# Splitting the weights later within the first four steps of a three-stage kernel on one core

## What is computed

```python
z = rmsnorm(x, norm_in_w) @ pre_w.T
folded = mean of z over 4 neighbouring tokens
gate = sigmoid(Hst @ harm_w.T + harm_b)
gfold = folded * gate
target = style @ style_w.T
cos = sum(l2norm(gfold) * l2norm(target))
cfg_blend = gfold + cfg * (1 + cos) * 0.5 * (target - gfold)
y = concatenate([x, cfg_blend]) @ merge_w.T + merge_b
h = gelu(rmsnorm(y, norm_out_w) @ ffn_w1.T + ffn_b1)
y = h @ ffn_w2.T + ffn_b2 + x
```

## Time and profile before

| what | value |
|---|---|
| device time, median of 3 runs | 1429.6 us (1429.23 to 1430.48) |
| the profiled execution's own time | 1431.61 us |
| its span, first to last instruction | 1429.8 us |
| mean granted TensorE clock | 0.987 |
| busy: PE, DVE, ACT, POOL | 1370.5, 960.7, 1035.9, 911.5 us |

### The profile page before, as it was taken

How to read it: one execution, slowest core, us unless ns; L and a number is a source line. 1 busy time by engine, 2 the same in 40 slices (tenths; PEclk the granted TensorE clock), 3 DMA queues, 4 the chain that set the end, 5 groups by cost and what they waited for, 6 DMA issues and landing times. The chain is left out here.

```text
span 1429.8 us, 30429 instructions
## 1 busy us (share of the span) xinstructions
PE 1370.5 (96%) x10795; PEld 1183.3 (83%) x10795; DVE 960.7 (67%) x2191; ACT 1035.9 (72%) x2703; POOL 911.5 (64%) x855
## 2 busy tenths in 40 slices
PE   7899999997899999999999999999999988999996
PEld 6799999996678887888888788788888777889896
DVE  5876667643776676677667667666755568678763
ACT  5556666565898889889888988988988732476662
POOL 2576666652678768867877876786787620354643
PEclk9899999999999999999999999999999999999999
DMA  5342222111100100110110011011011046145522
GB/s 159 114 129 67 68 67 68 49 45 30 38 9 30 53 23 31 53 45 9 52 46 31 30 53 36 18 53 45 9 45 46 30 148 253 45 104 156 137 35 30
DMA packets 61638, 89.04 MB, mean 62 GB/s; under 512 B 6144, under 2 KB 50992, under 8 KB 58800
## 3 DMA queue, kind: packets, MB, share of 16 engines
q1 hardware_dynamic: 53232, 75.82, 16.3%
q0 software_dynamic: 6144, 8.39, 3.6%
q10 hardware_dynamic: 2112, 2.88, 0.6%
HBM read 61.90 MB, written 25.18 MB: 61 GB/s over the span
## 5 line engine op out<-in xcount | busy, mean ns | idle before, releaser
L1386 POOL TENSOR_TENSOR prob<-prob,share_p 128x512 f32<-128x512 f32 x256 | 271.6, 1067 | 195.6 <-DVE share_p L1493 195.0
L1487 DVE TENSOR_REDUCE shift<-bank 128x2 f32<-128x512 f32 x256 | 164.7, 685 | 186.0 <-PE bank L1103 185.9
L1258 ACT ACTIVATE prob<-bank,shift 128x256 f32<-128x256 f32 x512 | 237.8, 479 | 64.3 <-DVE shift L1487 64.2
L147 PE MATMUL bank<-wqkv_h,rowsT_h 128*128 128x512 f32 x384 | 158.9, 414 | 2.8 <-PEq L311 1.7
L147 PE MATMUL bank<-wqkv_h,rowsT_l 128*128 128x512 f32 x384 | 151.5, 395 | 0.0
L147 PE MATMUL bank<-wqkv_l,rowsT_h 128*128 128x512 f32 x384 | 150.8, 393 | 0.0
L1115 PE MATMUL bank<-ident,prob 128*128 128x128 f32 x1024 | 142.7, 281 | 1.1 <-POOL prob L1386 1.1
L1374 POOL TENSOR_TENSOR landing<-landing,rq 128x512 f32<-128x512 f32 x128 | 131.1, 1046 | 8.4 <-DVE rq L1441 8.4
L1130 PE MATMUL bank<-pT,landing 128*64 128x256 f32 x1024 | 127.1, 388 | 1.7 <-ACT pT L1345 1.7
L1115 PEld LDWEIGHTS bank<-ident,prob 128*128 128x128 f32 x1024 | 109.5, 141 | 21.3 <-POOL prob L1386 3.7
L1258 ACT ACTIVATION_READ_ACCUMULATOR prob<-bank,shift 128x1 f32 x512 | 107.5, 210 | 0.0
(11 more groups left out here) (324 smaller groups left out, 4517.6 us busy)
## 6 DMA issues: line engine op xcount, KB each, us to landing
landing<-in_fc1s SPq DMA_DIRECT2D x6, 1024.0 KB
landing<-in_fc2s SPq DMA_DIRECT2D x6, 1024.0 KB
rows<-in_x SPq DMA_DIRECT2D x16, 256.0 KB, 2.9
xT<-in_xT SPq DMA_DIRECT2D x16, 256.0 KB, 2.7
x_again<-in_x SPq DMA_DIRECT2D x16, 256.0 KB, 2.8
x_rows<-x SPq DMA_DIRECT2D x16, 256.0 KB, 3.1
rows<-x_rows SPq DMA_DIRECT2D x16, 256.0 KB, 3.1
x<-x_rows SPq DMA_DIRECT2D x16, 256.0 KB, 2.9
```

What stands on the lines that cost most here:

```text
L147: last = nc.tensor.matmul(out, a, b, start=(n == 0), stop=(n == 3 * len(ks) - 1))
L1258: last = nc.scalar.activation(prob[at][:, n, :], score_bank[side][:, n * T:(n + 1) * T], ACT.Exp, bias=shift[:, at, n:n + 1], scale=-1.0, ...
L1386: nc.gpsimd.tensor_tensor(prob[at][:, :, :], prob[at][:, :, :], share[:, at, :].unsqueeze(2).to_broadcast([P, TT, T]), ALU.mult).then_inc( ...
L1487: nc.vector.tensor_reduce(shift[:, s % 2 * 2 + side, :], score_bank[side][:, :].rearrange("p (n m) -> p n m", n=TT), AX, ALU.min).then_inc ...
```

## The change

The instructions stay the same in number and in size; their places in the order of two engines change. On ScalarE the high part of piece 1 goes behind the squares of `gf` in step -2, that of piece 2 behind the copies to `xnT` in step -2, and that of piece 3 behind the copies to `xnT` in step -1. On VectorE the low part of piece 1 goes behind the blend in step -2, those of pieces 2 and 3 behind `hn` in steps -1 and 0, and `hbias` behind `bl_l` in step -2. TensorE, GpSimd and SyncE are untouched.

```diff
@@ -557,14 +557,12 @@
                     if at(t, -2):
                         act.wait_ge(gate_sum, 1)
                         nc.scalar.activation(gate[:, :, :], gate[:, :, :], ACT.Sigmoid).then_inc(gate_done, 1)
-                        high_part(act, 1)
-                        high_part(act, 2)
-                    if at(t, -1):
-                        high_part(act, 3)
                     if live(far):
                         wait(act, gf_done, 1, far, 1)
                         wait(act, g_rooted, 1, far - 1, 1)
                         squares(gf, junk_act[:, 1, :, :], g_sums).then_inc(gf_squared, 1)
+                    if at(t, -2):
+                        high_part(act, 1)
                     if live(new):
                         wait(act, xn_T, 1, new, 1)
                         wait(act, folded, 1, new - 1, 1)
@@ -572,6 +570,10 @@
                             last = nc.scalar.activation(xnT[:, k, 0:T], xn_bank[:, k * T:(k + 1) * T], ACT.Copy,
                                                         scale=cols[:, NORM_IN + k:NORM_IN + k + 1])
                         last.then_inc(xnT_out, 1)
+                    if at(t, -2):
+                        high_part(act, 2)
+                    if at(t, -1):
+                        high_part(act, 3)
                     if at(t, -3):
                         load_piece(act, 2)
                         load_piece(act, 3)
@@ -714,19 +716,8 @@
                     if at(t, -2):
                         dve.wait_ge(gate_done, 1)
                         link(nc.vector.tensor_scalar(gate[:, :, :], gate[:, :, :], 0.25, None, ALU.mult))
-                    if at(t, -2):
-                        low_part(dve, nc.vector, 1).then_inc(lo_pool, 1)
-                        dve.wait_ge(setup_done, 3)
-                        dve.wait_ge(tables_in, 32)
-                        for m in range(KT):
-                            last = nc.vector.tensor_scalar(hbias[:, m, :], banks[5][:, m * NB:(m + 1) * NB],
-                                                           cols[:, LN1_B + m:LN1_B + m + 1], cols[:, B_ADA + m:B_ADA + m + 1], ALU.add, ALU.add)
-                        last.then_inc(hbias_done, 1)
                     if at(t, -1):
-                        low_part(dve, nc.vector, 2).then_inc(lo_dve, 1)
                         dve.wait_ge(biases_in, 32)
-                    if at(t, 0):
-                        low_part(dve, nc.vector, 3).then_inc(lo_dve, 1)
                     if live(far):
 
                         wait(dve, pre_done, 1, far, 1)
@@ -797,12 +788,18 @@
                         for i in range(TT):
                             last = nc.vector.scalar_tensor_tensor(blend[:, i, :], trow_b[:, 0:D], mix[:, i:i + 1], gfs[:, i, :], ALU.mult, ALU.add)
                         last.then_inc(blended, 1)
+                    if at(t, -2):
+                        low_part(dve, nc.vector, 1).then_inc(lo_pool, 1)
                     if live(nxt):
                         wait(dve, y_rooted, 1, nxt, 1)
                         wait(dve, h_T, 1, nxt - 1, 1)
                         for i in range(TT):
                             last = nc.vector.tensor_scalar(hn[:, i, :], y[:, i, :], y_root[:, i:i + 1], None, ALU.mult)
                         last.then_inc(hn_done, 1)
+                    if at(t, -1):
+                        low_part(dve, nc.vector, 2).then_inc(lo_dve, 1)
+                    if at(t, 0):
+                        low_part(dve, nc.vector, 3).then_inc(lo_dve, 1)
                     if live(next_):
                         wait(dve, x_squared, 1, next_, 1)
                         nc.vector.tensor_scalar(x_sums[:, :], x_sums[:, :], 1.0 / D, RMS_EPS, ALU.mult, ALU.add).then_inc(x_ready, 1)
@@ -811,6 +808,13 @@
                         wait(dve, mrg_done, 1, nxt, 1)
                         nc.vector.tensor_tensor(bl_l[:, :, :].rearrange("p k t -> p (k t)"), bl_bank[:, :],
                                                 bl_h[:, :, :].rearrange("p k t -> p (k t)").bitcast(F32), ALU.subtract).then_inc(bl_lo, 1)
+                    if at(t, -2):
+                        dve.wait_ge(setup_done, 3)
+                        dve.wait_ge(tables_in, 32)
+                        for m in range(KT):
+                            last = nc.vector.tensor_scalar(hbias[:, m, :], banks[5][:, m * NB:(m + 1) * NB],
+                                                           cols[:, LN1_B + m:LN1_B + m + 1], cols[:, B_ADA + m:B_ADA + m + 1], ALU.add, ALU.add)
+                        last.then_inc(hbias_done, 1)
                     if live(old):
 
                         wait(dve, ffn2_done, TT, old, TT)
```

## The result

The changed kernel takes 1437.17 us (median of 5 runs, 1435.62 to 1437.73); the ratio to the kernel before is 1.0048, with a 95% interval of 1.0034 to 1.0063, or +6.9 us (4.9 to 9.0). It is slower, by half a per cent. The profiled execution has a span of 1435.4 us, 5.6 more than the one of before.

A forecast was written before the change was run, and what follows sets the result against it. TensorE was taken to bound the kernel from 57.3 us on, and VectorE's order up to `rowsT_l` before, in steps -2 and -1. Terms of 0.52 + 0.93 + 2.20 + 0.66 gave +4.3 us, 1433.9 us, range 1431.5 to 1437.0.

The forecast's parts named there:

- the sum: Steps -2 to 0: terms 1 to 4, 0.52 + 0.93 + 2.20 + 0.66, make +4.3 us.
- rival A: Longer pause ahead of `pre(1)` brings half clock to `pre(1)` and `merge(0)`: +0.5 to +2.1 us beyond the sum; chance 0.28.
- the forecast's own sign: Granted clock near 30 us: if 0.5, the forecast is wrong and rival A holds.
- Term 1: Step -2: merge's low part delays `x_sums`, the CAST meets `xT_l`, `rowsT_l` and `pre(1)` come 0.52 us later.
- Term 2: Step -1, ScalarE: w2's high part stands ahead of the squares of `y`, so `y_sums` comes 0.93 us later.
- Term 3: Step -1, VectorE: w1's low part behind `hn` stands ahead of `x_sums`, `bl_l` and `rowsT`: +2.20 us.
- Term 4: Step 0: w2's low part ahead of `x_sums` makes TensorE wait for `rowsT_l` at `pre(3)`: +0.66 us.
- B: ScalarE's and GpSimd's waits overlap more than counted; without terms 1 and 2 +2.9 us, 1432.5; chance 0.14.
- C: The low parts slip into waits that exist anyway, so the change does nothing: 1429.6 us; chance 0.08.
- D: Clock stays up in 42.6 to 47.1 and 53.9 to 57.3 us, low parts hidden: faster, 1425.3 us; chance 0.03.
- After step 3: Rest of the kernel behind `pre(3)`: claimed unchanged, any delay going on to the end whole.
- 1 us as the bound: Time after `pre(3)`: the forecast is wrong if it shrinks or grows by over 1 us.

The follow-up runs named there:

- step2_only: Kernel before with the edits of step -2 alone (merge and w1 high parts, merge low part, `hbias`); timed +1.9 us (0.6 to 3.3).
- fills: Kernel before plus products of the identity that feed nothing in TensorE's pauses of steps -1 and 0; 1429.46 us, ratio 0.9985.
- after_again: The changed kernel as it is, with a second profile and five more rounds; 1437.86 us, ratio 1.0041.
- pair at full clock: Kernel before and changed kernel, both with products that feed nothing in TensorE's pauses (fills and after_fills); ratios 0.9985 and 1.0030.
- hi3_back: Changed kernel with w2's high part back at the head of step -1 on ScalarE; timed +3.1 us (1.7 to 4.6).
- lo2_back: Changed kernel with w1's low part back at the head of step -1 on VectorE; timed +3.7 us (2.1 to 5.3).
- lo3_back: Changed kernel with w2's low part back at the head of step 0 on VectorE; timed +6.0 us (3.9 to 8.0).
- hi3_behind_y: Changed kernel with w2's high part behind the squares of `y` on ScalarE in step -1; timed +5.0 us (3.3 to 6.7).
- step2_back: Changed kernel with all edits of step -2 undone, those of steps -1 and 0 kept; timed +4.0 us (2.4 to 5.6).
- after_fills: Changed kernel with longer fills than fills, in TensorE's pauses from `pre(1)` to `pre(3)`; timed +4.3 us (2.7 to 5.7), ratio 1.0030.
- idle_pre1: Changed kernel with 14 products of the identity in place of 6 ahead of `pre(1)`; 1437.3 us, ratio 1.0043.
- gf_first: Kernel before with only w1's high part moved behind the squares of `gf` and the copies to `xnT`; timed -0.6 us (-2.0 to 0.7).

## Why the prediction was right, and where not

The forecast was slower, 1433.9 us, +4.3. It is slower, by more: +6.9 and +5.9 in two sets of runs. The range ended at 1437.0. The median of 1437.17 lies just above that; the ratio taken on 1429.6 gives 1436.5, inside. The mechanism held in each step of the sum, in size in the first three; the clock, which I had as rival A, came on top in the profiled executions of the changed kernel. By the forecast's own sign (the granted clock near 30 us) it was A: 0.55 from 29.7 to 33.1 us.

I had also taken 2.0 us off, since the profiled execution of the kernel before was that much above the median of its runs. The profiled execution of the changed kernel took 1437.17 us, which is the median itself. From profile to profile it is +5.6, and 1.3 more than the forecast's 1435.9. So a good part of the 3.3 us between 1433.9 and 1437.17 is this subtraction, which took one execution's excess for a fixed distance.

- **Term 1, +0.52**: `pre(1)` came 0.64 later, of which 0.14 is a later start of the whole trace (the first instruction of VectorE's step -2 is at 16.14 in place of 16.00). So 0.50; 0.52 in step2_only. The CAST met `xT_l`, 1.10 us. That is net of the 0.65 us for which `g_sums` waited in the trace of before. In fills, with the old order on ScalarE and w1 landing earlier, there was no such wait, and `pre(1)` came 12.24 us behind the first instruction of VectorE's step -2. In before it was 12.98 and in the changed kernel 13.48, so against an execution like that of fills the term is +1.24. I read the wait from one trace and took it for a property of the order.
- **Term 2, +0.93**: `y` to `y_sums` is 3.96 us, before 2.98: 0.98. What I had not seen is that 0.4 of it comes also without ScalarE: with the high part moved away, 3.37 to 3.39 us remain. The timeline shows 0.32 us of idling with no releaser between `xnT` and `dots` (37.02 and 37.52; their starts are 0.50 apart in place of 0.09). It is there in all eight kernels where w1's low part stands behind `hn`, and in none of the six where it stands at the head of the step. Its cause stays open. It makes w2's place on ScalarE worth 0.6, and w1's low part 0.4 more once ScalarE is out of the way.
- **Term 3, +2.20**: 12.27 against 10.07, 2.20.
- **Term 4, +0.66**: it was to be TensorE's wait ahead of `pre(3)`. That wait was 1.38 us in the changed kernel's profile and 0.48 in after_again's, in which the half clock lay otherwise. The distance shows 18.51 - 17.29 = 1.22 and 17.21 - 17.29 = -0.08. The pair at full clock gives 0.59, but in part by an entry that the term does not have (the low part at the head of step 0 holds `gf` up there), so that 0.59 is so near to 0.66 is partly luck. What held is that the CAST's 1.42 us are not met again: 0.41 in both profiles of the changed kernel.
- **The sum** is 0.50 + 0.98 + 2.20 + 0.59 = 4.3, the last term from the pair at full clock. With the later start (0.14), 1.52 at `pre(1)` and 0.63 behind `pre(2)`, 6.57 us: `pre(3)` came 6.57 later.
- **The clock (rival A, +0.5 to +2.1)**: at `pre(1)` it cost 1.5 us in four of the seven profiled executions with a pause of 2.2 us ahead of it (changed, after_again, hi3_back, step2_only) and nothing in three (lo2_back, lo3_back, hi3_behind_y). All seven have the same instructions in the same order up to there. In the seven in which the pause was shorter or filled it never fell on `pre(1)`; in two of these (step2_back, after_fills) it fell from 24.7 to 28.1 us, on the products of the identity just ahead. I gave A a chance of 0.28 and treated it as one case or the other; it differs from execution to execution. How often it comes in the timed runs is not known: both profiles of the changed kernel have it, and with the pause filled (idle_pre1) the time did not fall.
- **Rivals B, C and D** are out: terms 1 and 2 are there, nothing slipped into waits, and the half clock behind `pre(2)` stayed in all kernels without fills behind `pre(1)`.
- **After step 3** I expected an unchanged kernel. Within the first block that holds: the shift moves from 6.63 to 6.92 over ten steps. Later it does not. The shift of the changed profile is 6.75 us where attention begins to project, 5.15 at its end and 5.6 at the last instruction; that of after_again 7.6, 7.4 and 7.9. The same happens with the fills and with lo3_back, in either direction. The end of attention and the routing are short dependent stretches where the clock differs from execution to execution (0.91 over 1160 to 1180 us before, 0.74 over 1167 to 1187 in after_again). One place is shown: near 1120 us the shift of the changed profile falls by 0.6, where the kernel before had half clock from 1118.9 to 1122.3 us and the changed kernel had none. From `pre(3)` to the end the shift shrinks by 1.0 us in the changed profile (6.57 to 5.6) and grows by 2.9 in after_again (5.05 to 7.9); I had named 1 us as the bound beyond which I would be wrong. My statement that a delay goes to the end whole is thus wrong for one trace, by 1 to 3 us, and not shown for the timed runs.

What stays open: the timed +6.9 and +5.9 are 1.6 to 2.6 us above the 4.3 that the order costs in the traces, and filling the pause at `pre(1)` did not bring the median down. Two places are likely, and no run changed only one of them: the clock later in the kernel, as near 392 us in after_again, and w1 landing earlier in most executions of the kernel before than it did in the profiled one, which would make term 1 larger by some 0.7.

## What to carry to other kernels

A piece of one-off work belongs where its engine waits for another engine, and not behind "more urgent" work in the same step: here the low part of w1 was free at the head of its step, beside the products of TensorE, and cost its full 2.2 us in front of the operand that the next products wait for. That of w2 cost only a part of it, 0.6 us between the two kernels at full clock, where it was no longer free at the head either. Before counting on a wait as a gain, look for it in a second execution: the 0.65 us that the earlier squares were to give back stood in one trace of the old order and not in two others. Moving a wait off one engine's head is worth nothing if the next step in the chain starts on something else; follow it to the operand that the busiest engine waits for. When the pipeline fills and the pauses are short, products that feed nothing in those pauses can be worth more than a better order (2.1 us here, 1.0 to 3.4).

## What the runs showed of the hardware that was not expected

With the same instructions up to that point and the same pause of 2.2 us, TensorE's clock fell to 1.2 GHz in some executions and not in others, so a single profile can be 1.5 us off in each such place. A start 0.6 us sooner behind a pause (gf_first) gained next to nothing, because the half clock behind `pre(2)` lasted 1.0 us longer, which cost 0.5. The load of w1 let ScalarE start at 17.27, 17.62 or 18.09 us in three executions of the same order, and 0.65 us of VectorE's waiting came and went with it. And 0.32 us of idling on VectorE, with no releaser, came and went with the place of an instruction elsewhere in its program.
